# Constants and inner weights loaded in their final layout, and a new list of steps

## The chip, the cores and the metric

The kernel runs on one core of a Trainium2 chip. The core has a matrix engine (PE, with its weight loads shown apart as PEld), a vector engine (DVE), a scalar engine (ACT), a general engine (POOL) and a queue that only issues DMAs here (SP). They run unsynchronised, each through its own list of instructions in order, and meet at semaphores. The metric is the device time of one execution in microseconds.

## The reference, cut to what matters

One layer: attention with a test-time-trained memory, then a feed-forward block, each behind a layernorm with a residual. Four batches of 512 rows of 256 numbers are worked through in four chunks of 128 rows.

```python
attn_qkv = x @ Wqkv                       # x: layernormed, (4, 512, 256)
q, k = l2norm(heads(silu(...))), ...      # 4 heads of 64
lr = softplus(x @ Wlr + BASE_LR_INV); mom = sigmoid(x @ Wm + bm)
def step(carry, xi):                      # once a chunk, for 16 (batch, head) pairs
    out = (silu(q @ W0.T) * (q @ W2.T)) @ W1.T
    dw0, dw1, dw2 = gradients(k, v, W0, W1, W2, lr) + M * mean(mom)
    dw = newtonschulz5(dw)                # five times: A = X X^T; B = b A + c A A; X = a X + B X
    W = renorm(W + dw, row norms of the initial w)
ttt_out = rmsnorm(out) * o_norm_g * silu(x @ Ws + bs)
attn_out = softmax(windowed q k^T) @ v    # 2 heads of 128, window 128
x = x + layernorm((ttt_out + attn_out) @ Wo)
x = x + layernorm(gelu(layernorm(x) @ proj1.T + b1) @ proj2.T + b2)
```

All numbers are float32. The initial w0, w1 and w2 are the same for every batch.

## The kernel before, in words

The work is cut into some 690 steps, each named by kind, chunk and number (`NX.0.3.1`: the third product of Newton-Schulz, chunk 0, iteration 3, group 1). `ORDER` (line 136) is one written list of them. Every engine walks that list and emits its own share of each step, so that the list fixes the order on every engine, but not the timing between engines: that comes from semaphores. `bank_plan` (line 208) gives each step its PSUM banks from the same list, taking those that were free longest.

The kinds that matter here:
- `LN1`, `LNX`, `XT`: layernorm of a chunk's rows (DVE statistics, POOL for the root, DVE scaling), transposes on PE and a copy on ACT. `QK` and `VV` are the products with the weights, `SI` the silu on ACT, `NQ` and `NR` the norm of q and k (ACT square, DVE sum, POOL root, DVE reciprocal, POOL scaling), `TR` transposes of the results.
- `WI` and `WN`: row norms of the initial weights. `WX` transposes the inner weights on PE and copies them on ACT. `DH`, `FW`, `GB`, `OUT`, `DW` are the memory's forward and gradient products, `MU`, `MR`, `SS`, `SN` scale the gradient.
- `TX`, `NA`, `NB`, `NX`: one iteration of Newton-Schulz on one of three groups (w1, w2, w0). `TX` is four transposes copied by ACT; the others are 16 products of 64x64 in quarters of the PE array, read by DVE (`NA`, `NB`) or ACT (`NX`).
- `S`, `PT`, `PV`, `CT`, `WO`: windowed attention and output projection. `L2`, `NT`, `F1`, `F2`, `F2N`: layernorm and feed-forward.

ACT loads a table whenever a step needs another set of functions than the last (`table`, line 820): `SP` and `S` need one for exp and log, `SI`, `FW` and `GB` one for silu, `F1` one for gelu.

SP does not follow the list. It issues its DMAs as they are written (lines 461 to 503): the first rows of x, the weights, then twelve small constants and six pieces of w0, w1 and w2, and only then the rows of the second chunk (`rows_in(1)`), for which DVE waits in `LN1.1`. `WI` on DVE copies the six pieces out to all batches. PE starts with nine products on ones.

Of the kernel before, what the change touches and what calls it, by code (L numbers as in the profile page):

```python
# [40 lines left out]
SMALL = 5 * NH  # L41
LN_EPS = 1e-5
# [81 lines left out]
NOT_IN_FIRST = ("x_in", "ln1_stats", "ln1_mv", "ln1_var", "ln1_rstd", "xn", "xT_ps", "xnT", "mm_ps", "mm", "decayed")  # L124
# [4 lines left out]
def steps(text):  # L129
# [7 lines left out]
    LN1.0.0 XT.0.0 LNX.0.0 LN1.0.1 LN1.0.2 CO.0 LN1.0.3 LNX.0.1 QK.0.0 XT.0.1 LNX.0.2 LNX.0.3 VV.0.0 VV.0.1 SI.0.0  # L137
    NQ.0.0 XT.0.2 XT.0.3 QK.0.1 SI.0.1 WI.0 LN1.1 QK.0.2 VV.0.2 NQ.0.1 LNX.1 SI.0.2 NR.0.0 QK.0.3 VV.0.3 NR.0.1 NQ.0.2
    TR.0.0 SM.0 TR.0.1 SI.0.3 MS.0 NQ.0.3 TR.0.2 TR.0.3 XT.1 TR.0.4 TR.0.5 TR.0.6 TR.0.7 NR.0.2 NR.0.3 KL.0.0 KL.0.1
    KL.0.2 KL.0.3 SP.0 WX.0.0 WX.0.1 WX.0.2 S.0.0 S.0.1 VV.1.0 VV.1.1 TR.0.8 TR.0.9 WN.0 FW.0.0 FE.0.0 FE.0.1 DH.0  # L140
    FW.0.1 GB.0.0 GB.0.1 OUT.0.0 OUT.0.1 EL.0.0 EL.0.1 OE.0 QK.1.0 SI.1.0 QK.1.1 EY.0 SI.1.1 S.0.2 ELB.0.0 ELB.0.1
    PT.0.0 PT.0.1 MU.0.0 MU.0.1 MU.0.2 MR.0.0 MR.0.1 MR.0.2 QK.1.2 DW.0.0 DW.0.1 QK.1.3 SS.0.0 S.0.3 SS.0.1 OY.0
    VV.1.2 PV.0.0 PV.0.1 SS.0.2 PT.0.2 PT.0.3 SN.0.0 SN.0.1 VV.1.3 CT.0.0 PV.0.2 PV.0.3 SN.0.2 WO.0.0 TX.0.0.0
    TX.0.0.1 CT.0.1 NA.0.0.0 NA.0.0.1 SI.1.2 CT.0.2 WO.0.1 TX.0.0.2 NB.0.0.0 NB.0.0.1 CT.0.3 NA.0.0.2 NX.0.0.0
    NX.0.0.1 WON.0.0 WON.0.1 L2.0.0 NB.0.0.2 TX.0.1.0 WO.0.2 WO.0.3 NA.0.1.0 L2N.0.0 WON.0.2 WON.0.3 NX.0.0.2 SM.1
    L2.0.1 L2.0.2 TR.1.0 TX.0.1.1 TX.0.1.2 L2.0.3 TR.1.1 NA.0.1.1 NA.0.1.2 NB.0.1.0 L2N.0.1 L2N.0.2 L2N.0.3 TR.1.2
    TR.1.3 NB.0.1.1 NB.0.1.2 NT.0.0 MS.1 NT.0.1 NT.0.2 NT.0.3 NX.0.1.0 NX.0.1.1 NX.0.1.2 TX.0.2.0 NQ.1.0 TX.0.2.1
    TX.0.2.2 NQ.1.1 SI.1.3 F1.0.0 NA.0.2.0 NA.0.2.1 NA.0.2.2 F1.0.1 F1.0.2 LN1.2 NB.0.2.0 NB.0.2.1 NB.0.2.2 NQ.1.2
    NR.1.0 NR.1.1 F1.0.3 F1.0.4 LNX.2 NX.0.2.0 NX.0.2.1 NX.0.2.2 NQ.1.3 TX.0.3.0 TX.0.3.1 TX.0.3.2 F1.0.5 NA.0.3.0
    NA.0.3.1 WR.0 NA.0.3.2 XT.2 F1.0.6 NB.0.3.0 NB.0.3.1 NB.0.3.2 MM.1 NR.1.2 NR.1.3 NX.0.3.0 NX.0.3.1 NX.0.3.2  # L150
    TX.0.4.0 KL.1.0 TX.0.4.1 TX.0.4.2 F1.0.7 NA.0.4.0 NA.0.4.1 NA.0.4.2 KL.1.1 TR.1.4 TR.1.5 F2.0.0 SP.1 NB.0.4.0
    NB.0.4.1 MP.1 NB.0.4.2 TR.1.6 TR.1.7 TR.1.8 S.1.0 NX.0.4.0 NX.0.4.1 NX.0.4.2 RN.0.0 RN.0.1 RN.0.2 TR.1.9 RM.0.0
    RM.0.1 RM.0.2 F2.0.1 F2.0.2 DH.1 WX.1.0 WX.1.1 WX.1.2 F2.0.3 GB.1.0 EL.1.0 EL.1.1 KL.1.2 KL.1.3 GB.1.1 FE.1.0
# [80 lines left out]
def layer_kernel(nc, x, Wqkv, Wlr, Wm, bm, Ws, bs, Wo, w0, w1, w2, o_norm_g, qk_scale, qk_offset,  # L234
                 proj1T, proj1_bias, proj2T, proj2_bias, out):
    with ExitStack() as ctx:
# [31 lines left out]
        def halves(t):  # L268
# [15 lines left out]
        wsmall = wqkv[:, :, 3 * DIM:]  # L284
        small_bias = sb("small_bias", SMALL)
# [91 lines left out]
        w_in = share(X, 0, 3, 2, HD)  # L377
# [19 lines left out]
        ld_qkv, ld_small, ld_misc, ld_w, ld_p1, ld_p2, ld_wo = (sem(n) for n in (  # L397
            "ld_qkv", "ld_small", "ld_misc", "ld_w", "ld_p1", "ld_p2", "ld_wo"))
# [8 lines left out]
        MISC = 16 * 7  # L407
# [36 lines left out]
        def _(sp):  # L444
            for name in RAISED_AHEAD["sync"]:
                sp.sem_inc(S[name].sem)
            def rows_again(c):
# [50 lines left out]
            stores(1)  # L498
            rows_again(3)
            stores(2)  # L500
            stores(3)
# [1077 lines left out]
```

## Time and profile before

| | |
|---|---|
| median of 3 runs | 381.77 us (381.27 to 382.93) |
| span of the profiled execution | 380.1 us; 1.7 us less than the median, which counts what lies around the span |
| PE busy | 371.0 us, 98% |
| DVE, ACT, POOL busy | 257.6, 213.3, 193.9 us |
| ACT table loads | 22 of 1.283 us |
| HBM read, written | 7.73 MB, 2.10 MB |

The page gives the profiled execution no other time of its own than the span, from the first to the last instruction. A timeline row gives start, length, engine, line, what is written and read, shapes and a count; a bracket holds the idle time of the engine before it, and what ended it. A PE product of float32 counts as two instructions in the trace and as one in the list of the program. Lengths of pipelined products overlap; the distance between starts is what one costs.

### The profile page before, as it was taken

What the parts mean: (1) busy time and instruction counts of PE and PEld (TensorE: products, weight loads), DVE (VectorE), ACT (ScalarE), POOL (GpSimd) and SP (SyncE); (2) the same over time, 40 slices, a digit from 0 to 9 for tenths busy, and PEclk for the clock granted to TensorE, in tenths of its full rate; (3) what the DMA queues carried; (4) which work ended last, traced back from release to release, by engine and by line L of the source; (5) the groups of instructions that cost most, each with busy time, mean ns of one, the idle gap of its engine ahead of it and who ended that gap; (6) DMA issues with size and microseconds to landing.
All of it is one profiled execution on the core that took longest, in us unless ns stands there. A gap on an engine that the chain in (4) does not pass through costs nothing.

```text
span 380.1 us, 15979 instructions
## 1 busy us (share of the span) xinstructions
PE 371.0 (98%) x6760; PEld 295.4 (78%) x6760; DVE 257.6 (68%) x682; ACT 213.3 (56%) x432; POOL 193.9 (51%) x290
## 2 busy tenths in 40 slices
PE   8999999999999999999999999999999999999994
PEld 5588688856788877878578888688887757988883
DVE  4678998674278699898546746987875492767124
ACT  1799855766512766649743346665358575614500
POOL 4399865356239457475963434364333340557212
PEclk9999999999999999999999999999999999999999
DMA  5562200001000000000000200000000110000101
GB/s 156 121 238 60 83 1 6 3 3 46 16 3 2 3 3 2 3 4 5 16 19 17 71 16 3 2 2 17 20 3 4 40 36 2 0 3 0 57 0 55
DMA packets 12677, 10.84 MB, mean 29 GB/s; under 512 B 4544, under 2 KB 12096, under 8 KB 12608
## 3 DMA queue, kind: packets, MB, share of 16 engines
q1 hardware_dynamic: 12608, 9.83, 8.9%
q8 instruction: 54, 0.88, 1.0%
q14 instruction: 15, 0.12, 0.1%
HBM read 7.73 MB, written 2.10 MB: 26 GB/s over the span
## 4 chain that ended last, share of the span: by engine, by line
PE 86%; DVE 4%; SPq 3%; issue 2%; POOL 2%; ACT 1%; DMA 1%; POOLq 0%; DVEq 0%; ACTq 0%
PE pair L782 15%; PE pair L793 15%; PE pair L713 6%; PE pair L701 6%; PE pair L691 6%; PE pair L559 6%; PE pair L682 5%; PE pair L591 4%; PE pair L763 3%; PE pair L732 3%; PE pair L568 3%; PE pair L748 3%; PE pair L662 2%; PE pair L739 2%; PE pair L629 1%
## 5 line engine op out<-in xcount | busy, mean ns | idle before, releaser
L782 PE MATMUL pair<-xn2T,p1T 128*128 128x512 f32 (+1 forms) x160 | 59.1, 512 | 0.0
L793 PE MATMUL pair<-p2T,h 128*128 128x256 f32 x256 | 57.0, 379 | 0.0
L793 PEld LDWEIGHTS pair<-p2T,h 128*128 128x128 f32 x256 | 48.0, 190 | 6.4 <-issue 0.2
L1424 POOL TENSOR_SCALAR var<-mv 128x1 f32<-128x1 f32 (+1 forms) x55 | 13.1, 239 | 67.1 <-DVE mv L1382 37.4
L1034 ACT ACTIVATE h<-pair,b 128x512 f32<-128x512 f32 (+1 forms) x40 | 23.9, 602 | 36.0 <-PE pair L782 35.9
L782 PEld LDWEIGHTS pair<-xn2T,p1T 128*128 128x128 f32 x160 | 28.7, 190 | 17.1 <-issue 14.8
L1419 POOL TENSOR_TENSOR nq<-ssq,half 128x8 f32<-128x8 f32 (+1 forms) x16 | 24.2, 1513 | 27.5 <-DVE ssq L1141 27.5
L1056 DVE SCALAR_TENSOR_TENSOR A<-pair,eye 128x512 f32<-128x512 f32 x45 | 28.7, 683 | 13.2 <-PE pair L691 13.1
L1419 POOL TENSOR_TENSOR rstd<-var,neg_half 128x1 f32<-128x1 f32 (+1 forms) x55 | 33.5, 609 | 4.6
L1056 DVE SCALAR_TENSOR_TENSOR B<-pair,eye 128x512 f32<-128x512 f32 x45 | 28.9, 684 | 10.2 <-PE pair L701 10.0
L559 PE MATMUL pair<-wqkv,xnT 128*128 128x512 f32 x64 | 31.5, 627 | 0.6 <-ACT xnT L816 0.6
L701 PEld LDWEIGHTS pair<-A 64*64 64x64 f32 x1440 | 23.7, 134 | 7.5 <-issue 4.6
L987 ACT ACTIVATE masked<-masked,nmax 128x256 f32<-128x256 f32 (+1 forms) x32 | 15.1, 474 | 25.5 <-DVE nmax L1298 25.5
L823 ACT ACT_TABLE_LOAD x22 | 28.2, 1283 | 1.1 <-PEq L1569 0.7
L691 PEld LDWEIGHTS pair<-XT 64*64 64x64 f32 x1440 | 23.3, 134 | 6.3 <-issue 5.7
L816 ACT ACTIVATE XT<-pair 128x512 f32<-128x512 f32 x45 | 24.6, 600 | 6.4 <-PE pair L682 6.4
L713 PEld LDWEIGHTS pair<-X,B 64*64 64x64 f32 x1440 | 23.6, 134 | 5.0 <-issue 2.7
L959 ACT ACTIVATE X<-pair 128x512 f32<-128x512 f32 x36 | 19.8, 598 | 13.2 <-PE pair L713 13.1
L701 PE MATMUL pair<-A 64*64 64x64 f32 x1440 | 26.5, 221 | 0.3 <-issue 0.3
L713 PE MATMUL pair<-X,B 64*64 64x64 f32 x1440 | 26.1, 221 | 0.1
L691 PE MATMUL pair<-XT 64*64 64x64 f32 x1440 | 25.8, 221 | 0.3 <-ACT XT L816 0.2
L682 PE MATMUL pair<-ident,X 128*128 128x128 f32 x180 | 24.1, 276 | 0.5 <-ACT X L959 0.3
(165 smaller groups left out, 775.4 us busy)
## 6 DMA issues: line engine op xcount, KB each, us to landing
x_in<-in_L_attn_x_dram SPq DMA_DIRECT2D x16, 128.0 KB, 2.5
x<-in_L_attn_x_dram SPq DMA_DIRECT2D x16, 128.0 KB, 2.1
out_dram<-rows_a SPq DMA_DIRECT2D x16, 128.0 KB, 1.7
p1T<-in_L_ffn_proj_dram SPq DMA_DIRECT2D x1, 1024.0 KB, 4.7
p2T<-in_L_ffn_proj_dram SPq DMA_DIRECT2D x1, 1024.0 KB, 7.4
wqkv<-in_L_attn_Wqkv_dram SPq DMA_DIRECT2D x1, 768.0 KB, 4.8
wo<-in_L_attn_Wo_dram SPq DMA_DIRECT2D x1, 256.0 KB, 7.7
X<-in_L_attn_w_dram SPq DMA_DIRECT2D x6, 32.0 KB, 2.2
```

The lines of the kernel that those rows point to most:

```text
L559: mm_ = pe.matmul(ps, xnT[:, k, b * P:(b + 1) * P], wqkv[:, k, 0:512], start=(k == 0), stop=(k == KC - 1))
L682: mm_ = pe.transpose(ps[:, b * P:(b + 1) * P], X[:, g, 2 * b:2 * b + 2, :], ident[:, :])
L691: mm_ = pe.matmul(BANK[bank[0] + row][64 * col:64 * col + 64, n * HD:(n + 1) * HD], xt, xt, start=True, stop=True)
L701: mm_ = pe.matmul(BANK[bank[0] + row][64 * col:64 * col + 64, n * HD:(n + 1) * HD], a, a, start=True, stop=True)
L713: mm_ = pe.matmul(BANK[bank[0] + row][64 * col:64 * col + 64, n * HD:(n + 1) * HD], B[64 * row:64 * row + 64, g, 4 * (row ^ (slot & 1)) + ...
L782: mm_ = pe.matmul(ps[:, at], p1T[:, k, n * P:(n + 1) * P], xn2T[:, k, at], start=(k == 0), stop=(k == KC - 1))
L793: mm_ = pe.matmul(ps[:, 0:DIM], h[:, n, b * P:(b + 1) * P], p2T[:, n, :], start=(n == 0), stop=(n == HC - 1))
L816: return act.activation(dst, src, ACT.Copy)
L823: act.preload_act_table_set(name)
L1034: act.activation(h[:, n, at], BANK[bank[0]][:, at], ACT.Gelu, bias=b1[:, n:n + 1]).then_inc(S["h"].sem, 1)
L1056: return dve.scalar_tensor_tensor(out=out_, in0=in0, scalar=scalar, in1=in1, op0=op0, op1=op1)
L1419: return pool.tensor_tensor(out_, in0, in1, op)
```

## The change

- The three small weights join `Wqkv` in one load, as one array `Wall`. Seven constants come in one array `packed`, of 356 numbers per partition, into one tile. The host lays both out.
- The inner weights come in one array `states`, laid out as the kernel holds them for every batch, with their transposes: three loads of 768, 512 and 256 KB in place of six of 32 KB. The copies of `WI` on DVE go, and so do `WX.0.0` to `WX.0.2`.
- SP issues the rows of the second chunk right behind the constants, ahead of the inner weights. Later loads and stores (`XI`, `XA`, `F2N`) follow the list. `XA` for the third and fourth chunk waits until the outputs two chunks back are made.
- PE runs three products on ones, 64 columns wide, behind the first transposes.
- `ORDER` is a new list: the same steps but for the three `WX.0` that go and six that name SP's loads.

```diff
@@ sync @@
-            sp.dma_start(wqkv[:, :, 0:3 * DIM], Wqkv.rearrange("(k p) n -> p k n", p=P)).then_inc(ld_qkv, 16)
+            sp.dma_start(wqkv[:, :, :], Wall.rearrange("(k p) n -> p k n", p=P)).then_inc(ld_qkv, 16)
             for b in range(1, BATCH):
                 sp.dma_start(x_in[:, b, :], x[b, 0:CHUNK, :]).then_inc(first_x[b], 16)
-            sp.dma_start(wsmall[:, :, 0:12], Wlr.rearrange("(k p) n -> p k n", p=P)).then_inc(ld_small, 16)
...
-            sp.dma_start(b1[:, :], proj1_bias.rearrange("(k p) -> p k", p=P), allow_slow_non_contiguous=True).then_inc(ld_misc, 16)
-
-            sp.wait_ge(ld_qkv, 16)
-            for n, w in enumerate((w1, w2, w0)):
-                for i in range(2):
-                    sp.dma_start(w_in[64 * i:64 * i + 64, n, :, :], w[2 * i:2 * i + 2, :, :].rearrange("j r d -> r j d"))\
-                        .then_inc(ld_w, 16)
-            rows_in(1)
+            sp.dma_start(packed_in[:, :], packed).then_inc(ld_misc, 16)
+            XI(1)
+            sp.dma_start(W[:, :, :, :], states[:, 0:1536].rearrange("p (g s d) -> p g s d", s=8, d=HD)).then_inc(ld_w, 16)
+            sp.dma_start(WT02[:, :, :, :, :], states[:, 1536:2560].rearrange("p (b j k d) -> p b j k d", j=2, k=2, d=HD)).then_inc(ld_wT, 16)
+            sp.dma_start(W1T[:, :, :, :], states[:, 2560:3072].rearrange("p (b j d) -> p b j d", j=2, d=HD)).then_inc(ld_wT, 16)
             sp.wait_ge(*S["x_in"](1, 64))
@@ tensor, XT_ of chunk 0 @@
+                    if b == 0:
+                        for n in range(3):
+                            pe.matmul(BANK[7][:, 0:64], ones[:, :], ones[:, 0:64], start=True, stop=True)
@@ tensor, FW (GB and DH alike) @@
-                pe.wait_ge(*S["WT"](c, 3))
+                pe.wait_ge(*(S["WT"](c, 3) if c else (ld_wT, 32)))
@@ scalar, WI @@
-                act.wait_ge(*S["W"](0, 3))
+                act.wait_ge(ld_w, 16)
@@ vector @@
-                dve.memset(small_bias[:, 0:12], BASE_LR_INV)
...
-            def WI(c):
-
-                dve.wait_ge(ld_w, 96)
...
@@ ORDER, two of 40 lines @@
-    TX.0.4.0 KL.1.0 TX.0.4.1 TX.0.4.2 F1.0.7 NA.0.4.0 NA.0.4.1 NA.0.4.2 KL.1.1 TR.1.4 TR.1.5 F2.0.0 SP.1 NB.0.4.0
+    NA.0.2.2 SP.1 NB.0.2.0 NQ.1.2 F1.0.2 NR.1.1 NB.0.2.1 NR.1.2 NX.0.2.0 NQ.1.3 NR.1.3 F1.0.3 TX.0.3.0 F1.0.4
```

On ACT at the start of the program, before: `xnT` are the transposed rows (`XT`), `raw` the output of `QK`, `silu` of `SI`, `y` the squares of `NQ`, `B<-W` the squares of `WI`.

```order
L816 ACTIVATE raw<-pair 128x512 [waits s_silu,s_tr_ps,s_qk_ps]
L873 ACTIVATE silu<-raw 128x512 [waits s_klv,s_tr_ps,s_qk_raw,s_v_raw]
L874 ACTIVATE silu<-v_rows 128x2x2x64
L1022 ACTIVATE B<-W 128x256 [waits s_W]
L1022 ACTIVATE B<-W 128x256 x2
L816 ACTIVATE raw<-pair 128x512 [waits s_silu,s_tr_ps,s_qk_ps]
L886 ACTIVATE y<-silu 128x512 [waits s_silu]
```

The same place now:

```order
L874 ACTIVATE y<-silu 128x512 [waits s_comb,s_silu]
L804 ACTIVATE raw<-pair 128x512 [waits s_silu,s_tr_ps,s_qk_ps]
L861 ACTIVATE silu<-raw 128x512 [waits s_klv,s_tr_ps,s_qk_raw,s_v_raw]
L862 ACTIVATE silu<-v_rows 128x2x2x64
L804 ACTIVATE xnT<-pair 128x2x128 [waits s_first_xT]
L874 ACTIVATE y<-silu 128x512 [waits s_silu]
L804 ACTIVATE raw<-pair 128x512 [waits s_silu,s_tr_ps,s_qk_ps]
L1011 ACTIVATE B<-W 128x256 [waits ld_w]
L1011 ACTIVATE B<-W 128x256 x2
```

The squares now stand behind the third `raw`, not the second, and wait for the load of `W` itself.

On ACT in the first chunk's Newton-Schulz, before: `XT` and `X` are the copies of `TX` and `NX`, `h` the gelu of `F1`.

```order
L823 ACT_TABLE_LOAD
L1034 ACTIVATE h<-pair,b 128x512 x3
L886 ACTIVATE y<-silu 128x512
L1034 ACTIVATE h<-pair,b 128x512 x2
L959 ACTIVATE X<-pair 128x512 x3
```

The same place now:

```order
L811 ACT_TABLE_LOAD
L1023 ACTIVATE h<-pair,packed_in 128x512
L804 ACTIVATE XT<-pair 128x512 x3
L1023 ACTIVATE h<-pair,packed_in 128x512
L811 ACT_TABLE_LOAD
L837 ACTIVATE lr_exp<-lr_neg 128x48
L839 ACTIVATE lr_log<-lr_exp 128x48
L874 ACTIVATE y<-silu 128x512
L811 ACT_TABLE_LOAD
L1023 ACTIVATE h<-pair,packed_in 128x512
L948 ACTIVATE X<-pair 128x512
```

The exp and log of `SP.1` now stand between two gelus, with a table load on either side. In all the list has 29 table loads, where it had 22.

On PE in the same chunk's third and fourth iteration, before: `XT` is read by `NA`, `A` by `NB`, `X,B` by `NX`, `ident,X` by `TX`, `xn2T,p1T` by `F1`.

```order
L782 MATMUL pair<-xn2T,p1T 128x512 x4
L713 MATMUL pair<-X,B 64x64 x48
L682 MATMUL pair<-ident,X 128x128 x12
L782 MATMUL pair<-xn2T,p1T 128x512 x2
L691 MATMUL pair<-XT 64x64 x48
```

The same place now:

```order
L689 MATMUL pair<-A 64x64 x16
L670 MATMUL pair<-ident,X 128x128 x4
L770 MATMUL pair<-xn2T,p1T 128x512 x2
L701 MATMUL pair<-X,B 64x64 x16
L689 MATMUL pair<-A 64x64 x16
L679 MATMUL pair<-XT 64x64 x16
L579 MATMUL pair<-ident,silu 128x128 x4
L670 MATMUL pair<-ident,X 128x128 x4
```

Where the three groups went through each kind together, they are now one kind apart from each other. Runs of quarter products between full-array products number 62, where they numbered 53.

## Rows read from the trace of the kernel before

**Rows 1.** The profile page, its first lines.

```profile
span 380.1 us, 15979 instructions
PE 371.0 (98%) x6760; PEld 295.4 (78%) x6760; DVE 257.6 (68%) x682; ACT 213.3 (56%) x432; POOL 193.9 (51%) x290
```

**Rows 2.** The chain of waits of the first 40 us (start, us, what).

```profile
8.10 0.72 SPq L479
...
12.10 0.59 SPq L459
...
14.10 2.25 DMA x_in<-in_L_attn_x_dram
```

**Rows 3.** PE in order of time (start, us, engine, line, operands, count).

```profile
6.50 3.75 PE L559 MATMUL pair<-wqkv,xnT 128*128 128x512 f32 x4 [0.56 <-ACT xnT L816]
...
12.80 3.60 PE L559 MATMUL pair<-wqkv,xnT 128*128 128x512 f32 x8
...
25.17 1.47 PE L723 MATMUL pair<-ident,W 128*128 128x128 f32 x12
26.48 1.06 PE L732 MATMUL pair<-akT,aqT 128*128 128x128 f32 x8
27.37 2.03 PE L568 MATMUL pair<-wqkv,xnT 128*128 128x276 f32 x8
...
30.36 1.10 PE L629 MATMUL pair<-tttT,WT 64*64 64x128 f32 x32
...
36.29 3.70 PE L559 MATMUL pair<-wqkv,xnT 128*128 128x512 f32 x8
```

**Rows 4.** Busy us (instructions) of PE, PEld, DVE, ACT, POOL; PEclk, DMA share, GB/s.

```profile
8.00:9.00 1.00, 1.00 (x2) 0.34 (x1) 0.87 (x5) 0.00 (x0) 0.90 (x3) 1.00 0.19 68
```

**Rows 5.** DVE in order of time, at the start.

```profile
9.99 0.41 DVE L1087 TENSOR_SCALAR rows_b<-x_in,mv,rstd 128x256 f32<-128x256 f32 x1 [0.46 <-POOL rstd L1419]
```

**Rows 6.** ACT in order of time, at the start.

```profile
16.24 1.01 ACT L1022 ACTIVATE B<-W 128x256 f32<-128x256 f32 x3
...
28.44 1.08 ACT L816 ACTIVATE WT<-pair 128x512 f32<-128x512 f32 x2
...
31.05 1.28 ACT L823 ACT_TABLE_LOAD   x1
32.49 0.60 ACT L937 ACTIVATE B<-pair 128x512 f32<-128x512 f32 x1 [0.15 <-DVE row_ss L1365]
```

**Rows 7.** The page's DMA issues (count, KB each, median us to landing).

```profile
wqkv<-in_L_attn_Wqkv_dram SPq DMA_DIRECT2D x1, 768.0 KB, 4.8
```

**Rows 8.** POOL in order of time, at the start.

```profile
14.57 1.70 POOL L1419 TENSOR_TENSOR nq<-ssq,half 128x8 f32<-128x8 f32 x1 [4.62 <-DVE ssq L1141]
...
21.69 2.05 POOL L1419 TENSOR_TENSOR silu<-silu,rq 128x512 f32<-128x512 f32 x2
...
44.93 1.15 POOL L1419 TENSOR_TENSOR eye<-ident 128x64 f32<-128x64 f32 x4
```

**Rows 9.** The same view, of two stretches in the middle.

```profile
46.00:75.00 29.00, 28.59 (x698) 24.36 (x698) 25.24 (x72) 18.39 (x40) 15.02 (x27) 1.00 0.03 8
...
254.00:292.00 38.00, 37.23 (x1149) 32.30 (x1148) 28.68 (x73) 21.92 (x44) 13.68 (x28) 1.00 0.04 12
```

**Rows 10.** PE in order of time, in the middle.

```profile
92.43 1.63 PE L691 MATMUL pair<-XT 64*64 64x64 f32 x96
93.99 1.09 PE L543 MATMUL pair<-ident,rows_b 128*128 128x128 f32 x8
...
280.04 0.70 PE L701 MATMUL pair<-A 64*64 64x64 f32 x32
280.67 0.66 PE L591 MATMUL pair<-ident,raw 128*128 128x128 f32 x4
```

**Rows 11.** PE in order of time, third chunk; in brackets idle time and releaser.

```profile
287.33 0.63 PE L682 MATMUL pair<-ident,X 128*128 128x128 f32 x4 [0.33 <-ACT X L959]
```

**Rows 12.** DVE in order of time, at the end.

```profile
377.54 0.48 DVE L1056 SCALAR_TENSOR_TENSOR rows_a<-rows_a,rstd,x 128x256 f32<-128x256 f32 x1 [0.29 <-POOL rstd L1419]
```

More of the change, by code:

```diff
@@ L136 @@
 ORDER = steps("""
[L137 to L141, printed above, removed]
@@ new lines @@
+    OUT.1.0 FE.1.1 EL.1.1 OUT.1.1 ELB.1.1 XA.2 OE.1 QK.2.2 S.1.1 DW.1.0 MU.1.0 F2N.0.1 DW.1.1 MU.1.1 S.1.2
+    PT.1.0 QK.2.3 MR.1.0 MR.1.1 MU.1.2 PT.1.1 SS.1.0 S.1.3 PT.1.2 OY.1 MR.1.2 SS.1.1 VV.2.0 PV.1.0 SN.1.0 PV.1.1
+    SS.1.2 PV.1.2 SN.1.1 CT.1.0 PT.1.3 TX.1.0.0 WO.1.0 SN.1.2 CT.1.1 CT.1.2 WON.1.0 NA.1.0.0 TX.1.0.1 WO.1.1
+    PV.1.3 SI.2.0 NA.1.0.1 NB.1.0.0 VV.2.1 WON.1.1 TX.1.0.2 L2.1.0 CT.1.3 L2.1.1 WO.1.2 NX.1.0.0 NB.1.0.1
+    NA.1.0.2 WON.1.2 TX.1.1.0 WO.1.3 SI.2.1 L2N.1.0 TR.2.0 L2N.1.1 NX.1.0.1 NB.1.0.2 L2.1.2 NA.1.1.0 WON.1.3
@@ L231, with layer_kernel @@
 PLAN = bank_plan(ORDER)
-def layer_kernel(nc, x, Wqkv, Wlr, Wm, bm, Ws, bs, Wo, w0, w1, w2, o_norm_g, qk_scale, qk_offset,
-                 proj1T, proj1_bias, proj2T, proj2_bias, out):
+def layer_kernel(nc, x, Wall, packed, states, Wo, proj1T, proj2T, out):
     with ExitStack() as ctx:
@@ L485, in _, with run @@
             sp.dma_start(wo[:, :, :], Wo.rearrange("(k p) n -> p k n", p=P)).then_inc(ld_wo, 16)
-            rows_again(0)
-            def stores(c):
-                for b in range(BATCH):
-                    sp.wait_ge(*S["outb"](c, b + 1))
-                    sp.dma_start(out[b, bass.ts(c, CHUNK), :], outb[:, b, :]).then_inc(S["stored"].sem, 16)
-            rows_again(1)
-            rows_in(2)
-            rows_in(3)
-            stores(0)
-            rows_again(2)
[L498 to L501, printed above, removed]
+            def run(order):
+                for kind, c, *arg in order:
+                    if kind in parts:
+                        parts[kind](c, *arg)
+            run(ORDER)
             sp.wait_ge(*S["stored"](CHUNKS, 0))
@@ L1555, in _, with laid_out, rows, lanes @@
             run(ORDER)
-_INS = ['L0_attn_x', 'L0_attn_Wqkv', 'L0_attn_Wlr', 'L0_attn_Wm', 'L0_attn_bm', 'L0_attn_Ws', 'L0_attn_bs', 'L0_attn_Wo',
-        'L0_attn_w0', 'L0_attn_w1', 'L0_attn_w2', 'L0_attn_o_norm_g', 'L0_attn_qk_scale', 'L0_attn_qk_offset',
-        'L0_ffn_proj1', 'L0_ffn_proj1_bias', 'L0_ffn_proj2', 'L0_ffn_proj2_bias']
+_INS = ['L0_attn_x', 'Wall', 'packed', 'states', 'L0_attn_Wo', 'L0_ffn_proj1', 'L0_ffn_proj2']
 _TRANSPOSED = ('L0_ffn_proj1', 'L0_ffn_proj2')
+def laid_out(name, inputs):
+    if name == 'Wall':
+        return np.concatenate([np.asarray(inputs['L0_attn_' + n]) for n in ('Wqkv', 'Wlr', 'Wm', 'Ws')], axis=1)
+    if name == 'packed':
+        def rows(a):
+            return np.broadcast_to(np.asarray(a), (P, np.asarray(a).size))
+        def lanes(a):
+            return np.asarray(a).reshape(-1, P, int(np.prod(np.asarray(a).shape[1:]))).transpose(1, 0, 2).reshape(P, -1)
+        return np.concatenate([rows(np.full(3 * NH, BASE_LR_INV, np.float32)), rows(inputs['L0_attn_bm']), rows(inputs['L0_attn_bs']),
+                               lanes(inputs['L0_ffn_proj1_bias']), rows(inputs['L0_ffn_proj2_bias']), rows(inputs['L0_attn_o_norm_g']),
+                               lanes(inputs['L0_attn_qk_scale']), lanes(inputs['L0_attn_qk_offset'])], axis=1)
+    if name == 'states':
+        w = [np.asarray(inputs['L0_attn_' + n]) for n in ('w1', 'w2', 'w0')]
+        t = [a.transpose(0, 2, 1) for a in w]
+        half = range(2)
+        W = np.stack([np.stack([np.concatenate([w[g][2 * i + (j ^ (b & 1) if g == G_W1 else j)] for i in half])
+                                for b in range(BATCH) for j in half], axis=1) for g in range(3)], axis=1)
+        WT02 = np.stack([np.concatenate([t[g][2 * j + i] for i in half])
+                         for b in range(BATCH) for j in half for g in (G_W0, G_W2)], axis=1)
+        W1T = np.stack([np.concatenate([t[G_W1][2 * j + (i ^ (b & 1))] for i in half])
+                        for b in range(BATCH) for j in half], axis=1)
+        return np.concatenate([a.reshape(P, -1) for a in (W, WT02, W1T)], axis=1)
+    return inputs[name].T if name in _TRANSPOSED else inputs[name]
 def kernel(**inputs):
```

144 lines of the change are left out of this document (66 added, 78 removed).

## The prediction

> **What bounds the kernel now.** I read the page first: PE is busy for 371.0 of 380.1 us, and DVE, the next, for 68% [rows 1]. A busy PE is not yet a PE at its pace, so I then read PE's timeline by the distance between starts. At its best pace a group of 96 quarter products costs 1.56 us [rows 10] and an instruction of 512 columns 0.45 us [rows 3]. Counting every piece at the best pace of its kind leaves, as an estimate, 2.6 of the 29 us from 46 to 75 and 3.8 of the 38 us from 254 to 292 over, under 1.3 us in any other stretch behind 14 us; these are the stretches where DVE is busy for 87% and 75% [rows 9]. So PE bounds the kernel, and what can be won is PE work taken away, the first 30 us, and those two stretches.
>
> The first 30 us have another bound. The chain of waits goes through SP there: it still issues pieces of w0 to w2 at 8.10, issues the second chunk's rows from 12.10, and their last one takes from 14.10 to 16.35 to land [rows 2]. DVE sits in that wait in order, with the bias sums behind it, and ACT's silu behind those.
>
> I make the sum against the profiled execution's span, 380.1 us; the median of 381.77 lies 1.7 us above it.
>
> **PE work that goes.** WX.0 is 12 transposes, from 25.17 to 26.48: 1.31 us of PE with nothing idle around it [rows 3]. Its three copies on ACT go too (two of them are 1.08 us [rows 6], so about 1.5 us), beside PE, but on an ACT that has no idle time in that stretch.
>
> **The start.** The rows of the second chunk are issued once the fourth `xn` is made, at 10.40 before [rows 5]; the new DVE order puts that at about 10.6. That is 1.5 us ahead of 12.10, so they land near 14.85. What is late next:
> - ACT waits in WI.0 for the load of W. It is issued behind four DMAs that took from 12.10 to about 14.5 before (the last starts to travel at 14.10 [rows 2]), so at about 13.0. A load of the same 768 KB took 4.8 us [rows 7], which gives 17.8; at the 385 GB/s that the wqkv load moved at its peak it would be 16.5. ACT came to its WI at 16.24 before [rows 6] and comes at about 16.1 now. The wait costs 0.4 to 1.7 us; I take 1.0. Before, the copies on DVE were there in time.
> - POOL: the root of the norm takes 1.70 us, two scalings 2.05 [rows 8]. The new list puts the second and third root ahead of the second scaling. From rows at 14.85, DVE's statistics 1.8 and POOL's root of them 1.3, one scaling (1.0), and two roots with their sums (2 x 2.0) come to 22.9, and the scaling that TR.0.7 waits for ends at 23.9; the last scaling ends at 28. PE cannot go through TR.0.9 before.
> - From 28.0, PE has TR.0.9 (0.5 us) and what stood from 30.36 to 36.29 before (FW, DH, FW, GB, OUT [rows 3]), less DH (0.9), which comes ahead of it now: 5.5 us, so it ends OUT.0.1 at about 33.5. Before, it was there at 36.29, with VV.1.0 and VV.1.1 done, which now come later (2.03 us long, some 0.15 of it beside the next piece [rows 3]: 1.9). So the start gives 36.3 - 1.9 - 33.5 = 0.9 us, the 1.31 us of WX.0 within it, of which the rest is taken back by the two waits. Bounds: nothing, if W lands at 17.8 and POOL runs 0.6 us later than that; 2.5 us, if only the earlier rows count (1.5 us) with most of WX.0 on top.
> - The four `eye` additions (1.15 us [rows 8]) move from POOL's busy stretch to one in which it stood idle for 4.62 us: nothing, at most 1.15 us.
>
> The three products on ones fill the 0.56 us in which PE waited ahead of the first QK [rows 3], so they cost nothing; outside that hole they would cost about 0.6 us. The first QK's four pieces take 3.75 us, eight later ones 3.60 [rows 3]: 1.2 GHz against 2.4, though the column of the granted clock reads 1.00 there [rows 4]. If the clock rises at 6.5, QK.0.0 ends 1.8 us earlier; but the next silu waits for DVE's and POOL's layernorms of batch 1, and the whole is behind W's wait on ACT, so I count 0 here, and 0.7 us at most either way.
>
> A rule bears on this. "TensorE: Matmul & The Clock Gate" of the Trainium skill (Part 4, PE-mode transpose) says that transposes do not count as activity for the clock. By it the transposes ahead of the products on ones leave their part of the hole open, and the clock may rise no earlier. In this trace the clock stayed low through ones, transposes and QK alike, so it cannot tell.
>
> The small loads (`Wall` is 3% more bytes, `packed` 182 KB, `states` 1.5 MB where 0.2 MB were) land before their readers but for W, above. In words of time: at the same rate all of `states` is 4 us of transfer, in front of p1T, p2T and wo, which PE needs from 53 us on.
>
> **SP's new order.** XA.2 waits for all four outputs of the first chunk, and three stores stand behind it. Four loads one after the other, 2.25 us each [rows 2], and three stores make 12 us; the next reader, F2.1.0 on DVE, comes 21 us of PE work later. Nothing; without that cover, up to 12 us once.
>
> **The list in the middle.** Three terms.
> - Covers. From TX to NA and from NX to TX a copy on ACT lies between, and PE was seen idle for 0.33 us where too little work covered it [rows 11]. Counting PE work between source and reader at the paces above, 26 of 168 such places in Newton-Schulz had under 1.0 us before, 12 have now; the attention pieces of the first chunk (CT to WO 0.9 us before, 2.5 now) look alike. Of the 6.4 us over in the two stretches I take half as won: 3.3 us. Bounds: 0 and 6.4.
> - Runs of quarter products. A run of 96 costs 1.56 us, a run of 32 0.63 [rows 10]: 0.465 for each 32 and 0.165 for the run. Nine more runs cost 1.5 us. Bounds: 0.5 to 2.
> - Table loads. Seven more of 1.28 us [rows 6] are 9.0 us of ACT, which is 56% busy. The one around SP.1 puts two loads, exp, log, a square and two gelus (5.5 us) between two copies of Newton-Schulz; PE has some 8 us of products in between, two F1 among them. I count 0. Bounds: 0 to 9.0.
>
> A rule speaks against this. "ScalarE: Activation LUTs" (What ACT_TABLE_LOAD costs) gives 1.28 us for the load and 1.38 us more of drain for each switch. The trace has 1.28 us, with the next activation 0.16 us later, and that one waited for DVE [rows 6]; the measurement decides. By the page seven switches would be 18.6 us of ACT.
>
> **The end.** The last DVE row starts at 377.54 [rows 12], behind the last F2; the steps of the last chunk are the same there. Nothing.
>
> **Sum.** -0.9 at the start, -3.3 for the covers, +1.5 for the runs: -2.7, so a span of 377.4 and a time of 379.1 us. Its own range is 376.5 to 380.8.
>
> **Rivals.**
> - The list wins nothing: excess in the two stretches is DVE's load (87% busy [rows 9]), which no order takes away; the covers' gain just pays for the runs. Then only the start counts, 0 to 1.3 us, 0.9 at the value above: 380.9. For it: DVE's share. Against it: the stretch at 150 to 180 is as loaded, and has 1.2 us over.
> - Slower: ACT's table loads come through. In Newton-Schulz each one stands ahead of a copy that PE waits for, and ACT goes in order. Each that is not covered adds 1.28 us to 379.1: from four on (384.2) the kernel is measurably slower, with all seven it is 388.1. I price it at four, 384.2. For it: 29 loads for 22, two of them around each split of F1 in the second and third chunk. Against it: F1 (1.8 us of PE) stands next to most of them.
> - The whole excess goes: 6.4 us won, 1.5 paid, 2.5 at the start: 381.8 - 6.4 + 1.5 - 2.5 = 374.4. For it: all covers grow. Against it: DVE.
> - The ones do not do what they are there for: the clock still rises near 10 us, every chain of the start 0.7 us later: 379.8. Nothing in the trace speaks against it, and by the rule on transposes it is what would happen.
>
> **Chances.** Forecast 0.44, the list wins nothing 0.24, slower 0.15, whole excess 0.07, clock no earlier 0.10. What a measurement can tell from no change is 0.5%, 1.9 us: below 379.9 is faster. Of the forecast 0.42 is faster, of the whole excess all, of the clock's case half: 0.54. Slower is 0.15 and 0.01 of tails: 0.16. The rest, 0.30, is the same. The range takes in the whole excess at its low end, and the slower case only up to two or three uncovered loads: 374.6 to 383.6.
>
> **What would show it.** The first row of LN1.1 on DVE near 14.9; an idle ACT ahead of its squares of W, ended by the DMA, of 0.4 to 1.7 us; QK.0.0's four pieces in 1.9 us if the ones work, 3.75 if not; PE at the end of OUT.0.1 near 33.5. In the middle no wait of PE for ACT over 0.5 us, and the time between the first chunk's TX.0.0.0 and the last F2 of the third chunk shorter by 2 us. The prediction is wrong where PE waits right behind a table load, or where the two stretches keep their excess.

## The result, and the profile after

The changed kernel takes 387.19 us (median of 4 runs, 385.92 to 387.65) against 381.69 (381.27 to 382.93) before: a ratio of 1.0136, 95% interval 1.0118 to 1.0154. It is 5.5 us slower; I had forecast 379.1. The page of the profiled execution, its span and busy times, then the share of the engines in the chain that ended last, against [rows 1]:

```profile
span 385.1 us, 15948 instructions
PE 372.1 (97%) x6754; PEld 295.6 (77%) x6754; DVE 258.9 (67%) x675; ACT 224.6 (58%) x436; POOL 198.3 (51%) x290
q8 instruction: 54, 0.88, 1.0%
PE 92%; issue 1%; DVE 0%; POOLq 0%; POOL 0%; DVEq 0%
```

The span grew by 4.9 us and PE's busy time by 1.1. So the chain is still PE's, with more standing still in it. PE's waits in the whole program (what waited for what, us in total, times, longest), over 0.3 us:

```profile
PE pair L579 <- ACT raw L804: 2.6, 1, 2.6
PE pair L579 <- issue: 1.2, 1, 1.2
PE pair L796 <- DVE ones L1043: 1.0, 1, 1.0
PE pair L522 <- DVE rows_b L1075: 0.9, 2, 0.5
PE pair L679 <- issue: 0.9, 2, 0.7
PE pair L701 <- issue: 0.6, 2, 0.4
PE pair L689 <- issue: 0.4, 1, 0.4
```

Two things stand out: 2.6 us for ACT's copy of QK's output (once, at the start), and waits "for issue", in which PE waited for nothing that the profile names. None is a wait for ACT's copies in Newton-Schulz.

**The start.** ACT's and DVE's first waits, then PE from 16 us, then the granted clock by microsecond (the columns are length, then busy time and count of PE, PEld, DVE, ACT, POOL, then PEclk, DMA share, GB/s):

```profile
17.84 1.03 ACT L1011 ACTIVATE B<-W 128x256 f32<-128x256 f32 x3 [2.08 <-DMA W<-in_states_dram]
14.58 1.41 DVE L1065 BATCH_NORM_STATS2 st<-x_in 128x6 f32<-128x256 f32 x4 [1.17 <-DMA x_in<-in_L_attn_x_dram]
```

```profile
16.47 1.88 PE L548 MATMUL pair<-wqkv,xnT 128*128 128x512 f32 x4
20.98 3.39 PE L579 MATMUL pair<-ident,raw 128*128 128x128 f32 x16 [2.63 <-ACT raw L804]
24.17 2.16 PE L579 MATMUL pair<-ident,silu 128*128 128x128 f32 x16
26.17 1.04 PE L532 MATMUL pair<-ident,rows_b 128*128 128x128 f32 x8
35.54 1.98 PE L548 MATMUL pair<-wqkv,xnT 128*128 128x512 f32 x4
```

```profile
20.00:21.00 1.00, 0.02 (x1) 0.05 (x1) 0.73 (x3) 1.00 (x4) 0.89 (x2) 1.00 1.00 413
21.00:22.00 1.00, 1.00 (x6) 1.00 (x7) 0.47 (x5) 0.95 (x3) 0.85 (x1) 0.63 1.03 383
22.00:23.00 1.00, 1.00 (x7) 1.00 (x6) 0.00 (x0) 1.00 (x2) 0.91 (x2) 0.50 1.10 362
24.00:25.00 1.00, 1.00 (x8) 1.00 (x7) 0.03 (x1) 1.00 (x2) 1.00 (x2) 0.66 1.11 353
25.00:26.00 1.00, 1.00 (x12) 1.00 (x11) 0.94 (x2) 0.98 (x2) 0.91 (x2) 1.00 0.43 139
```

The rows of the second chunk are there at 14.58, as planned. But ACT stands 2.08 us for W, its next `raw` comes late, PE stands 2.63 us for that, and then PE's clock falls from its full level (2.4 GHz) to half of it: TR.0.0 to TR.0.3 take 3.39 us where 16 such products took 1.94. OUT.0.1 ends at 35.54. Before it was 36.29 with VV.1.0 and VV.1.1 done (1.9 us), so 34.4 on the same footing [rows 3]: the start is 1.15 us later, where I had forecast 0.9 earlier.

**The waits for issue.** PE's timeline around the longest of them, and what the chain that ended last makes of the same place:

```profile
65.15 0.56 PE L701 MATMUL pair<-X,B 64*64 64x64 f32 x21
66.07 0.45 PE L701 MATMUL pair<-X,B 64*64 64x64 f32 x11 [0.35 <-issue]
...
69.95 0.27 PE L579 MATMUL pair<-ident,raw 128*128 128x128 f32 x1
71.46 0.98 PE L579 MATMUL pair<-ident,raw 128*128 128x128 f32 x7 [1.23 <-issue]
...
264.81 0.29 PE L679 MATMUL pair<-XT 64*64 64x64 f32 x6
265.77 0.40 PE L679 MATMUL pair<-XT 64*64 64x64 f32 x13 [0.68 <-issue]
```

```profile
65.22 0.49 PE pair L701 x21
65.72 0.35 issue
66.07 0.45 PE pair L701 x11
...
70.12 0.11 PE pair L579
70.23 1.23 issue
71.46 0.98 PE pair L579 x7
```

They stand in the middle of a group, between two products that need the same data, so a semaphore is hardly what PE waits for; `e5` and `e6` below test that. I counted the PE instructions recorded ahead of each (products, weight loads and separate waits): 1472, 1728, 1984, 6592, 10176, 10688 and 12480. Each is 192 more than a multiple of 256. The page has a queue named "instruction" that moves 54 packets in 0.88 MB, 16 KB each; PE's 13,900 recorded instructions make 54 blocks of 256, which puts an instruction at 64 bytes (`e6` below has 14,043, and 55 packets). One such packet falls shortly ahead of the long wait (the DMA view from 66 to 74, in 40 slices of 0.2 us):

```profile
DMA  0000000000000000200000000000000000020000
GB/s 0 0 0 0 0 0 0 0 0 0 0 0 0 0 0 0 82 0 0 0 0 0 0 0 0 0 0 0 0 0 0 0 0 0 0 82 0 0 0 0
q8 instruction: 2, 0.03, 1.5%
```

The packet starts at 69.23 and is in at 70.15; PE goes on at 71.46. PE had come to the end of the block before at 65.50 and to the end of this one at 69.95, 4.45 us later; the packet started 3.73 us behind 65.50, took 0.92, and PE went on 1.31 behind its end: 5.96 us in all, 1.5 too late. At all seven places PE went on 1.3 to 1.4 us behind the end of such a packet. So PE came to the end of a block of its instructions before the next one had arrived. Taking the distance between two starts there less that of their neighbours, the seven waits make 4.3 us, and 4.65 with two smaller places at such a count; in the kernel before there is one, 0.38 us, at 261.6.

### The profile page after: what moved, and what is told of

Read it like the earlier page. It is cut to its first block, busy times and chain, and to the rows that moved or that the text cites. A ratio compares the mean times of both kernels' runs of the same rounds, so it can differ in the third digit from the quotient of the medians.

```text
span 385.1 us, 15948 instructions
## 1 busy us (share of the span) xinstructions
PE 372.1 (97%) x6754; PEld 295.6 (77%) x6754; DVE 258.9 (67%) x675; ACT 224.6 (58%) x436; POOL 198.3 (51%) x290
## 4 chain that ended last, share of the span: by engine, by line
PE 92%; issue 1%; DVE 0%; POOLq 0%; POOL 0%; DVEq 0%
PE pair L770 15%; PE pair L781 14%; PE pair L701 7%; PE pair L689 6%; PE pair L679 6%; PE pair L670 6%; PE pair L548 6%; PE pair L579 5%; PE pair L751 4%; PE pair L720 3%; PE pair L736 3%; PE pair L556 3%; PE pair L650 2%; PE pair L617 2%; PE pair L727 2%; PE pair L592 2%
## 5 line engine op out<-in xcount | busy, mean ns | idle before, releaser
L1045 DVE SCALAR_TENSOR_TENSOR B<-pair,eye 128x512 f32<-128x512 f32 x45 | 30.5, 683 | 15.7 <-PE pair L689 15.7
L1023 ACT ACTIVATE h<-pair,packed_in 128x512 f32<-128x512 f32 (+1 forms) x40 | 24.0, 602 | 24.8 <-PE pair L770 24.6
L1394 POOL TENSOR_TENSOR rstd<-var,neg_half 128x1 f32<-128x1 f32 (+1 forms) x55 | 33.5, 609 | 4.6
L701 PEld LDWEIGHTS pair<-X,B 64*64 64x64 f32 x1440 | 25.1, 134 | 10.7 <-issue 8.2
L701 PE MATMUL pair<-X,B 64*64 64x64 f32 x1440 | 29.9, 222 | 0.7 <-issue 0.6
L689 PE MATMUL pair<-A 64*64 64x64 f32 x1440 | 29.5, 220 | 0.4 <-issue 0.4
L679 PE MATMUL pair<-XT 64*64 64x64 f32 x1440 | 29.0, 220 | 0.9 <-issue 0.9
L689 PEld LDWEIGHTS pair<-A 64*64 64x64 f32 x1440 | 25.2, 135 | 6.0 <-issue 5.6
L679 PEld LDWEIGHTS pair<-XT 64*64 64x64 f32 x1440 | 24.8, 135 | 5.3 <-issue 4.9
L670 PE MATMUL pair<-ident,X 128*128 128x128 f32 x180 | 26.5, 278 | 0.0
L1353 DVE TENSOR_TENSOR rows_a<-pair,packed_in 128x256 f32<-128x256 f32 x16 | 6.7, 419 | 25.4 <-PE pair L781 25.4
```

The lines of the kernel that those rows point to most:

```text
L670: mm_ = pe.transpose(ps[:, b * P:(b + 1) * P], X[:, g, 2 * b:2 * b + 2, :], ident[:, :])
L679: mm_ = pe.matmul(BANK[bank[0] + row][64 * col:64 * col + 64, n * HD:(n + 1) * HD], xt, xt, start=True, stop=True)
L689: mm_ = pe.matmul(BANK[bank[0] + row][64 * col:64 * col + 64, n * HD:(n + 1) * HD], a, a, start=True, stop=True)
L701: mm_ = pe.matmul(BANK[bank[0] + row][64 * col:64 * col + 64, n * HD:(n + 1) * HD], B[64 * row:64 * row + 64, g, 4 * (row ^ (slot & 1)) + ...
L1023: act.activation(h[:, n, at], BANK[bank[0]][:, at], ACT.Gelu, bias=b1[:, n:n + 1]).then_inc(S["h"].sem, 1)
L1045: return dve.scalar_tensor_tensor(out=out_, in0=in0, scalar=scalar, in1=in1, op0=op0, op1=op1)
```

## The experiments

The theory: the list of steps costs some 4 us behind the start, by waits at the ends of PE's blocks, and the rest is lost at the start, by the wait for W. The rivals: the loads cost it; or the waits belong to the steps in which they stand; or ACT's table loads. Each kernel was timed over five rounds beside the kernel before (381.96 to 382.1 us in these runs).

**Which half of the change.** `e1` is the new code with the old list, WX.0 taken out, SP's steps put in:

```diff
-ORDER = steps("""<new list>""")
+ORDER = steps("""<old list without WX.0.*, with XA.0 XA.1 XI.2 XI.3 behind OE.0, XA.2 behind F2N.0.3, XA.3 behind F2N.1.3>""")
```

> The new loads, constants and ones with the list of the kernel before (WX.0 taken out of it, SP's loads put in). Theory A, the list is what costs: the middle is as before, WX.0 is gone (-1.3 us), and ACT, which comes to its squares of W earlier than W lands (17.8 us), waits some 2 us there and gives the gain back: 380 to 383 us. Theory B, the loads are what costs (768 KB of W late, 1.5 MB ahead of p1T): 385 us or more, whatever the list.

383.82 us, ratio 1.005 (1.0037 to 1.0062). That is 0.8 us above theory A's range and 1.2 below theory B's: nearer to A, and 3.4 us less than the changed kernel.

`e2` is the old code with the new list (`WX.0.0 WX.0.1 WX.0.2` ahead of `DH.0`, SP's steps taken out):

> The code and loads of the kernel before with the new list (WX.0 put back ahead of DH.0). Theory A: the new list loses about 4 us behind the start and nothing waits for a late W: 385 to 388 us. Theory B: 381.7 us, as before, within 1 us.

390.87 us, ratio 1.0237 (1.0209 to 1.0265): more than theory A allowed. DVE waits 2.34 us for the second chunk's rows there (to 16.43), ACT 4.05 us for DVE's copies of W behind them, and PE stands 5.08 us ahead of TR.0.0; the first piece behind OUT.0.1 starts at 40.23. The new list needs the new loads at the start, and is slower with either behind it.

**The two repairs.** `e3` moves one step of the new list; `e4` keeps the new list to OUT.0.1 and takes the remaining steps in the old order; `e9` does both; `e10` is `e1` with the move:

```diff
-    ... NQ.0.1 QK.0.2 WI.0 VV.0.2 ... TR.0.1 TR.0.2 TR.0.3 NR.0.2 ...
+    ... NQ.0.1 QK.0.2 VV.0.2 ... TR.0.1 TR.0.2 TR.0.3 WI.0 NR.0.2 ...
```

> The changed kernel with one step moved in the list: WI.0, ACT's squares of W, behind TR.0.3 instead of ahead of the third silu. Theory A: ACT's 2.08 us wait for W goes, with it PE's 2.63 us ahead of TR.0.0 and the fall of the granted clock to 0.50 behind it; the start ends 2 us earlier: 385.2 us, TR.0.0 to TR.0.3 in about 2.0 us instead of 3.39. Rival: POOL's roots and scalings are late next (the last scaling that TR.0.9 waits for ends at 28.8 us) and keep the start where it is: 386.5 to 387.2 us.

385.37 us, ratio 1.0079 (1.005 to 1.0108), 1.8 us less than the changed kernel: theory A's time. W's wait is gone, the clock stays at 1.00 and the four TR take 1.94 us, but PE still stands 1.34 us ahead of TR.0.0 and 1.18 for POOL's scaling, and ACT has a new wait of 1.70 us for DVE's bias sums, which stand behind the wait for the second chunk's rows. The block-end waits are where they were.

> The changed kernel with its own list up to OUT.0.1 and the steps that are left in the order of the list before. Theory A, the list behind the start costs 4 us: 383.3 us, with 383 to 384 holding it. Rival: the stalls in the middle of groups (1.2 us at 70, 0.7 at 265) come from the program or the chip and not from the order of the steps: 385.5 to 387 us, and such stalls are in this trace too.

383.11 us, ratio 1.0035 (1.0018 to 1.0053): theory A. Taken from the medians, the order behind OUT.0.1 alone costs 4 us. One long block-end wait is left (0.8 us, at 60). Part of the 4 us can lie in the start, which differs between executions of the same instructions: W landed at 17.33 in this profile, the clock stayed at 1.00, and OUT.0.1 ended at 34.63, 0.9 us earlier than in the changed kernel's. The nine runs fall into five with a mean granted clock of 0.997 or more, 382.5 us on average, and four at 0.993, 384.2; the changed kernel's four are at 0.992 to 0.996. Like with like, the order costs 3 to 4 us.

> The changed kernel's loads and start, WI.0 moved behind TR.0.3, and behind OUT.0.1 the order of the list before: the two repairs together. Theory A: 383.1 less the 1.8 us that the first repair gave on the whole new list: 381.3 us, 380.8 to 382. Rival: POOL's chain holds the start, 382.5 to 383.1.

382.56 us, ratio 1.0008 (0.9996 to 1.0021): the rival. With the old rest the move gives only 0.5 us; the profile has ACT idle for 2.33 us behind DVE's bias sums in place of W, as the second chunk's rows landed at 15.24 in it, against 14.51 in `e3`'s.

> The new loads with the list of the kernel before, and WI.0 behind TR.0.3. The old list with the new loads took 383.8 us with ACT waiting some 2.5 us for W. Theory A, that wait goes and nothing is late in its place: 382 us. Rival: DVE waits for the second chunk's rows ahead of the bias sums that ACT's silu needs, so that ACT stands idle there instead, as in the new list with WI.0 late (1.7 us): 383.3 to 383.8 us.

381.01 us, ratio 0.9975 (0.9965 to 0.9984), 1 us less than theory A had. This beats the kernel before by 1 us, and the changed one by 6. ACT's wait for the bias sums is only 0.44 us here, and PE goes into TR.0.0 without idle time, at 18.96.

**Whose waits are they.** `e5` and `e6` put 16 and 32 tiny products into PE's idle time ahead of TR.0.0 of the changed kernel; `e7` 10 full ones:

```diff
@@ tensor, TR, behind take(...) @@
+                    if c == 0 and u == 0:
+                        for n in range(16):      # e6: 32; e7: 10 of ps[:, 0:P], ones[:, :], ones[:, :]
+                            pe.matmul(ps[0:32, 0:32], ones[:, 0:32], ones[:, 0:32], start=True, stop=True)
```

> The changed kernel with 16 tiny products on ones (32x32, about 1 us) put ahead of TR.0.0, in PE's idle time there: nothing else changes but that each later PE instruction stands 64 places further on. Theory A, PE waits for its own instructions where it comes to the end of a block of 256: the waits in the middle of groups (at after's 60.4, 65.5, 70.0, 177.3, 264.9, 274.3, 304.1 us, 4.5 us together) go from those instructions and stand 64 instructions earlier in the list, again where the number of recorded PE instructions ahead is 192 more than a multiple of 256; their sum changes, by up to 2 us either way, and the time with it. Rival, the waits belong to the step in which they stand (a semaphore, a bank, a neighbour's work): they stay in the same places, and the time is 387.2 us within 0.5.

389.06 us, ratio 1.0193 (1.0167 to 1.0219). The wait in TR.1.1 is gone. PE's timeline has one elsewhere, where the changed kernel had none:

```profile
80.28 0.41 PE L692 MATMUL pair<-A 64*64 64x64 f32 x16
81.98 0.46 PE L692 MATMUL pair<-A 64*64 64x64 f32 x16 [1.28 <-issue]
```

> The same with 32 tiny products, 128 places (about 2 us in an idle time of 2.6). Theory A: the waits stand 128 instructions earlier in the list than in the changed kernel, with another sum. Rival: the same places, 387.2 us within 0.5.

385.8 us, ratio 1.0111 (1.009 to 1.0131). Other places again. In both, every wait over 0.15 us inside a group stands at 192 more than a multiple of 256, and their sums are 6.0 and 3.0 us. The rival is out: the waits went from their steps and stand at the same counts again. The time moved by 1.9 us one way and 1.4 the other; of these only the first is clear of the noise (the intervals of `e6` and of the changed kernel overlap). The clock stayed at 1.00 in both, too, and the start ended 0.9 and 0.4 us earlier.

> The changed kernel with 10 full products on ones (128x128, about 2.2 us) ahead of TR.0.0, so that PE does not stand idle for 2.6 us. Theory A, the idle time lowers the granted clock: it stays at 1.00, TR.0.0 to TR.0.3 take 1.94 us instead of 3.39, and the kernel gains at most 1.4 us where PE is what the start waits for, less where POOL's last scaling at 28.8 us is: 386.0 to 387.0. Rival, the clock falls for another reason: 3.39 us and 387.2 us. Blocks of 256 instructions shift by 40 places as well, which may move the time by 2 us either way; the trace tells the two apart.

387.67 us, from 385.69 to 391.07, ratio 1.0154 (1.012 to 1.0189). The granted clock stayed at 1.00 and the four TR took 1.97 us, as theory A had it; the time is above its range, as the gain is lost in the block-end waits, 9 us in the profiled execution (389.3 us), the highest sum seen. That execution was the slowest of the six, and 5.4 us lie between it and the fastest: the waits differ between executions of one kernel too. So the price of the clock is read from the traces here, not from the time.

**Can the ends of the blocks be put back.** `e12` is `e9` with 9 tiny products (above, `range(9)`):

> The new start with WI.0 late and the old order behind it (382.6 us), with 9 tiny products on ones ahead of TR.0.0. The kernel before had 12 transposes more and 3 products on ones less ahead of the middle, so that these 9 put the ends of PE's blocks of 256 instructions where they stood before. Theory A: the waits at the blocks' ends fall from 1.7 us to about 0.4, as before, and the time to 381.3 us (380.8 to 381.8). Rival, where the blocks end makes no difference in the old order: 382.6 us.

382.4 us, ratio 1.0008 (0.9999 to 1.0017): a miss, with waits of 2.0 us behind the start and not 0.4. But it does not test what it was made for. A transpose leaves two records in the trace where a product leaves four. The first piece of F1 stands 2455 recorded PE instructions in before, 2438 in `e9`, and 2473 in `e12`: 17 were missing, and 9 products put in twice that. So no run has the new loads and the blocks ending where they did before. What bears on the question is that `e1`, `e4`, `e9` and `e10` have the same order behind the start and the same count there (2438), and their waits make 0.2 to 1.7 us; `e8`, below, has the order and the counts of the kernel before, and 1.3 us of waits for its 0.4. The same ends in the same order do not fix the waits.

**Table loads.** `e8` is the kernel before with more of them:

```diff
@@ scalar, TX @@
+                if g == 0:
+                    act.preload_act_table_set(loaded[0])
                 act.wait_ge(*S["xt_ps"](c, 3 * it + g + 1))
```

> The kernel before with 15 more table loads on ACT, one ahead of the first of the three copies of TX in each iteration of Newton-Schulz of the first three chunks. My prediction counted seven more loads at nothing. Theory A, a table load on ACT is covered as long as PE has other products: 0 to 2 us more, 382 to 384 us. Rival, each stands between PE and the copy it waits for: 15 x 1.28 = 19 us, or half of it, 391 to 401 us.

387.73 us, ratio 1.0148 (1.0132 to 1.0165): 5.8 us for 15 loads, 0.4 us each, between the two. Its profile shows what an uncovered load looks like, and the changed kernel's has no such row:

```profile
PE pair L691 <- ACT XT L816: 3.6, 5, 1.1
```

**The ones.** `e13` takes out the three products on ones and puts three tiny ones ahead of TR.0.0:

> The changed kernel without the three products on ones behind the first transposes, and with three tiny ones ahead of TR.0.0, so that the blocks end at the same instructions. Theory A, the three products raise the clock earlier in some executions, but the start waits for POOL, DVE and W, not for QK.0.0: 387.2 us within 0.5. Rival: with the first QK at half the clock (3.75 us for its four pieces) the start is up to 0.7 us later: 387.7 to 388.

386.45 us, ratio 1.0103 (1.0088 to 1.0119), no slower than with them, and a little under theory A's range. The late start of its profile (36.8 in the table below) goes with a late W: it landed at 19.37, and ACT stood 3.50 us for it. QK.0.0 ran in 1.96 us all the same:

```profile
6.23 1.96 PE L545 MATMUL pair<-wqkv,xnT 128*128 128x512 f32 x4 [0.57 <-ACT xnT L804]
```

**All kernels in one table.** Start is where PE begins behind OUT.0.1 (less 1.9 us where VV.1.0 and VV.1.1 are done by then); block ends is the sum of the waits at counts of 192 more than a multiple of 256 behind the start, worked out from the distances between PE's starts; rest is the span less both. All in us, of the profiled executions.

| kernel | list behind start | span | start | block ends | rest |
|---|---|---|---|---|---|
| before | old | 380.1 | 34.4 | 0.4 | 345.4 |
| after | new | 385.1 | 35.5 | 4.7 | 344.9 |
| e1 new loads, old list | old | 381.9 | 35.6 | 0.9 | 345.4 |
| e2 old loads, new list | new | 387.5 | 40.2 | 2.7 | 344.6 |
| e3 WI.0 late | new | 383.1 | 34.0 | 4.4 | 344.7 |
| e4 old rest | old | 380.5 | 34.6 | 1.2 | 344.7 |
| e5 shift 64 | new | 386.4 | 34.6 | 6.0 | 345.8 |
| e6 shift 128 | new | 383.4 | 35.1 | 3.0 | 345.3 |
| e7 fill | new | 389.3 | 35.0 | 8.9 | 345.4 |
| e8 15 table loads | old | 386.7 | 34.2 | 1.3 | 351.2 |
| e9 e3 and e4 | old | 381.5 | 34.7 | 1.7 | 345.1 |
| e10 old list, WI.0 late | old | 379.1 | 33.7 | 0.2 | 345.2 |
| e12 e9 shifted | old | 381.1 | 34.6 | 2.0 | 344.5 |
| e13 no ones | new | 385.1 | 36.8 | 4.0 | 344.4 |

But for e8 the rest is 344.4 to 345.8 whatever the list. The two other columns carry all the differences. The block ends cost 2.7 to 8.9 us (seven kernels) with the new list, 0.2 to 2.0 (seven) with the old one. Each is one execution, and the 8.9 comes from the slowest of `e7`.

## Why the prediction was wrong, point by point

- **What bounds the kernel.** PE does, as I said. But I took each stretch's time over the best pace as waits for other engines or as DVE's load. PE can also wait for its own instructions, and the sum has no term for it. This is the step that failed: of the 4.9 us of span 4.3 are block-end waits. Of the 7.7 us between the forecast span (377.4) and the measured one they are the larger part too; the start is 2.05 (0.9 forecast as gain, 1.15 measured as loss), covers and runs together 1.3 (1.8 forecast, 0.5 seen).
- **WX.0.** 1.31 us of PE forecast. By the distance between starts, transposes of W in the whole program take 5.38 us before and 3.93 after: right.
- **Start, rows.** LN1.1's first row at 14.58, forecast 14.9: right.
- **Start, W.** Taken at 1.0 us, with a range of 0.4 to 1.7; it was 2.08. W landed at 17.8, the late end of my range, and ACT came 0.3 us earlier than I counted. What I did not follow was its consequence on PE: 2.63 us idle, and behind it the clock. PE lost 1.45 us on the four TR alone. The last scaling on POOL ended at 28.77, not 28.0, TR.0.9's group began at 29.22, and OUT.0.1 ended at 35.54, not 33.5. My bound at the bad end was "nothing"; it was a loss of 1.15. The fall of the clock is some 0.7 us of that: in `e3` to `e6`, all at 1.00, OUT.0.1 ended 6.0 to 6.1 us behind POOL's last scaling, in the changed kernel and `e13`, where it fell, 6.8. W landed later in `e5` (18.22) than in the changed kernel, and OUT.0.1 ended at 34.64 all the same.
- **Start, what is late next.** POOL's last scaling, as I said. Moving WI.0 (e3) brought its end to 27.95, forecast 28.0, and OUT.0.1's to 34.02. The 0.5 us over the forecast are PE's work behind it: 6.07 us, where I had counted 5.5.
- **Ones.** No cost: right. They are not what makes QK.0.0 fast: it took 1.95 us with them and 1.96 in e2 and e13 without. The slow QK.0.0 before (3.75 us [rows 3]) belongs to that one execution: in `e8`, with the same start and no such products, it took 1.98. They may help where the clock is still low at 5.3 us (the nine first products then took 4.21 us, and QK.0.0 1.94 in e1 and e4), but only one trace without them, that of before, shows the other side. No measurable time hangs on it.
- **Covers.** -3.3 us forecast (0 to -6.4). From the table's last column, covers and runs together gave 0.5 us (345.4 to 344.9), and over all kernels nothing that stands out. The covers did their work where PE was seen to wait: before, it stood for copies or scalings of ACT and DVE at 67, 133, 256 and 287 us (0.19, 0.44, 0.18 and 0.33), and none of these is left. That is 1.1 us; what took more than half of it back is not shown. The excess from 46 to 75, without block-end waits, stayed at 2.3 us (2.5 before), and that from 254 to 292 is 3.1 before and 3.0 now, as an estimate of the same kind, as the rival "the list wins nothing" had it. Whether it is DVE's load, as that rival said, no run shows.
- **Runs of quarter products.** +1.5 us forecast. The quarter products of Newton-Schulz take 73.4 us before and 76.2 after, of which the block-end waits that stand in them are 0.4 and 3.0: 0.2 us is left for nine more runs, or 0.5 if the wait at 287 us, which stood in them before, is set against it. The 0.165 us for a run, from the two groups of [rows 10], was at least three times too large; perhaps the piece beside it gains what one piece loses there.
- **Table loads.** 0 forecast, and 0 seen: PE waits for no copy of ACT behind the start. e8 shows that loads are not free wherever they stand. The rule that I weighed, in "ScalarE: Activation LUTs" of the Trainium skill (What ACT_TABLE_LOAD costs), 1.38 us of drain for each switch, isn't seen here either; the rows below have the next activation 0.01 us behind the load:

```profile
25.26 1.28 ACT L811 ACT_TABLE_LOAD   x1
26.55 0.24 ACT L837 ACTIVATE lr_exp<-lr_neg 128x48 f32<-128x48 f32 x1
```

- **SP's order and the end.** No wait of PE for a DMA and the same last steps: nothing, as forecast.
- **The rivals.** 384.2 for "slower" had the right side by the wrong mechanism. None named block ends, and with the range ending at 383.6 the measured time lay outside it.

What stays open is why blocks arrive late in the new list. In the changed kernel five packets between 58 and 78 us start 1.9 to 3.7 us after PE came to the end of a block, with the kernel before 0.5 to 1.7 for the same five, and e3 repeats the late ones within 0.2 us. It isn't the order and the count alone (`e1`, `e4`, `e9` and `e10` share them), nor other DMA traffic, of which there are only two packets of 8 KB there, in both kernels. What triggers a packet I could not see in a trace, and did not try to change.

## What to carry to other kernels

A kernel of thousands of small PE instructions can run so near to the rate at which they are fetched that reordering it moves the time by 1%, with no wait that a dependency explains (here 3 to 4 us for the order, 1.9 us for 16 tiny products more); in the trace, look for idle time "for issue" inside a group, count the instructions ahead of it, and compare the counts. When a wait is taken away, follow the one it hides: here the load of W, then the rows of the next chunk through DVE's in-order queue. And test a new list and new loads apart: the loads with the old list and one step moved were the faster kernel.

## What the runs showed of the hardware

- PE's instructions arrive in packets of 16 KB during the run, 54 in each trace (55 in `e6`), each 0.9 to 1.7 us long; in the changed kernel PE went on 1.3 to 1.4 us behind the end of a late one. "Trainium Architecture — The Big Picture" of the Trainium skill (The software stack) has the instruction streams brought into each engine's memory when the program is loaded; the trace disagrees, with packets from 27.5 to 361 us in the changed kernel.
- The granted clock fell to 0.50 behind an idle PE in three traces: 2.63 us idle (after), 3.66 (e13) and 5.08 (e2). Behind 2.59 us idle in e1 and 1.1 to 2.0 in e3 to e6 it stayed at 1.00, and in e7, where products filled the idle time down to 0.43 us and W landed as in the changed kernel.
- In the windows above it came back from 0.50 to 1.00 between 22 and 25 us, in a stretch in which PE did transposes alone. By "TensorE: Matmul & The Clock Gate" of the Trainium skill (Part 4, PE-mode transpose) transposes do not count as activity for the clock, and it would have stayed low at least until the first other product, at 27.13; it was at 1.00 from 25 on. So it rose behind nothing but these float32 transposes, which the trace shows as products with the identity. In e2 it is the same: 0.50 from 27 to 28 us, 1.00 from 29, with nothing but transposes from 23.35 to 31.67.
